# Four layers in one kernel: attention image by image, stacks copied inside SBUF, and a layer on 32x32 tiles

## What is computed

```python
x = x + _L0_conv_ref(_gn(x), W1, W2, bias_w)     # a Volterra convolution, 9 linear and 45 product features
x = x + _L1_conv_ref(_gn(x), weight, bias)       # a convolution by FFT, of the kernel summed over its outputs
x = x + _L2_conv_ref(_gn(x), ...)                # attention in a recurrent cell, below
x = x + _L3_conv_ref(_gn(x), weights1)           # Hartley transform, mix of modes, transform back
```

```python
xin = jnp.einsum('nchw,oc->nohw', x, W_in) + b_in[None, :, None, None]
...
    q = _conv(query, Wq[idx], 'SAME').reshape(n, HEADS, HC, -1)
    k = _conv(token, Wk[idx], 'VALID').reshape(n, HEADS, HC, -1)
    v = _conv(token, Wv[idx], 'VALID').reshape(n, HEADS, HC, -1)
    w = jax.nn.softmax(jnp.einsum('nhcq,nhcd->nhqd', q, k), axis=-1)
    a = jnp.einsum('nhcd,nhqd->nhcq', v, w).reshape(n, CA, hh, ww)
```

## Time and profile before

| engine | busy in us of the span of 337.9 | instructions |
|---|---|---|
| PE, matmul | 311.3 (92%) | 2827 |
| PE, weight load | 120.5 (36%) | 2827 |
| DVE | 208.7 (62%) | 472 |
| ACT | 178.0 (53%) | 337 |
| POOL | 33.4 (10%) | 35 |

### The profile page before, as it was taken

One profiled execution on the slowest core, in us unless ns is written; L12 is line 12 of the kernel. 1 busy time (PEld: TensorE's weight loads), 2 busy tenths in 40 slices (PEclk: granted clock), 3 DMA queues, 4 the chain that ended last, 5 costly groups with the idle time before them and its releaser, 6 DMA issues.

```text
span 337.9 us, 7025 instructions
## 1 busy us (share of the span) xinstructions
PE 311.3 (92%) x2827; PEld 120.5 (36%) x2827; DVE 208.7 (62%) x472; ACT 178.0 (53%) x337; POOL 33.4 (10%) x35
## 2 busy tenths in 40 slices
PE   5999989999988999999999999999999899977793
PEld 1689523234322223323323223322232222423751
DVE  4970362577288337686868878867787221477364
ACT  1100101135185768787887969888788788300400
POOL 6910400000000000100101001010010100000000
PEclk9999978999896569999999999999999999997798
DMA  7000000005650854750000000000000000000001
GB/s 257 31 4 4 2 0 0 3 0 151 161 121 18 157 132 113 278 250 3 2 3 0 3 2 2 0 2 4 2 0 2 2 3 0 0 2 1 4 2 62
DMA packets 3756, 15.05 MB, mean 45 GB/s; under 512 B 804, under 2 KB 1572, under 8 KB 3308
## 3 DMA queue, kind: packets, MB, share of 16 engines
q1 hardware_dynamic: 3468, 14.50, 14.7%
q0 software_dynamic: 256, 0.11, 0.2%
HBM read 12.13 MB, written 2.37 MB: 43 GB/s over the span
## 4 chain that ended last, share of the span: by engine, by line
PE 79%; DVE 12%; issue 4%; ACT 3%; DMA 1%; ACTq 0%; DVEq 0%
PE ps L1151 16%; PE ps L1133 16%; PE ps L1110 15%; PE ps L998 9%; PE ps L1060 3%; PE ps L1254 3%; PE ps L960 2%; PE ps L1048 2%; ACT arena_b L638 2%; PE ps L1156 2%; PE ps L1209 2%; PE ps L1034 2%; PE ps L1026 1%; PE ps L969 1%; DVE arena_a L921 1%
## 5 line engine op out<-in xcount | busy, mean ns | idle before, releaser
L638 ACT ACTIVATE arena_b<-ps 128x512 f32<-128x512 f32 x232 | 125.4, 605 | 32.3 <-PE ps L1133 31.3
L1110 PE MATMUL ps<-arena_a 72*128 72x450 bf16 x256 | 89.3, 378 | 1.4 <-DVE vrest L811 0.8
L1133 PE MATMUL ps<-arena_a 75*128 75x512 bf16 x224 | 86.7, 397 | 0.7 <-ACT arena_b L638 0.3
L846 DVE TENSOR_REDUCE mx<-ps 128x1 f32<-128x450 f32 x120 | 69.3, 618 | 6.8 <-PE ps L1110 5.8
L841 DVE CUSTOM_DVE_ANT_0 sums<-ps,relus 128x450 bf16<-128x450 f32 x68 | 41.3, 626 | 35.7 <-PE ps L1110 29.7
L1151 PE MATMUL ps<-arena_b,vt 128*32 128x512 f32 x448 | 61.4, 621 | 0.7 <-ACT arena_b L638 0.7
L1133 PEld LDWEIGHTS ps<-arena_a 75*128 75x128 bf16 x224 | 21.9, 99 | 72.5 <-ACT arena_b L638 43.9
L646 ACT ACTIVATE relus<-ps 128x450 f32<-128x450 f32 x68 | 37.3, 552 | 7.0 <-PE ps L1110 7.0
L1110 PEld LDWEIGHTS ps<-arena_a 72*128 72x128 bf16 x256 | 24.2, 101 | 36.9 <-DVE mx L841 9.4
L960 PE MATMUL ps<-zeros 128*128 128x512 bf16 x76 | 21.2, 425 | 4.4 <-DMA xa<-x 3.9
L998 PE MATMUL ps<-arena_b,arena_a 32*32 32x512 f32 x720 | 24.6, 610 | 0.0
(11 more groups left out here) (135 smaller groups left out, 240.8 us busy)
## 6 DMA issues: line engine op xcount, KB each, us to landing
arena_b<-wmodes SPq DMA_DIRECT2D x1, 4096.0 KB, 13.3
arena_a<-k_scratch SPq DMA_DIRECT2D x9, 258.4 KB
arena_a<-q_scratch SPq DMA_DIRECT2D x12, 96.0 KB
arena_a<-q_scratch SPq DMA_DIRECT2D x3, 384.0 KB
k_scratch<-arena_b SPq DMA_DIRECT2D x3, 344.5 KB, 3.3
cst<-consts SPq DMA_DIRECT2D x1, 967.5 KB, 7.8
arena_a<-k_scratch SPq DMA_DIRECT2D x6, 129.2 KB
q_scratch<-arena_b SPq DMA_DIRECT2D x6, 128.0 KB, 4.8
```

The source lines that it names most:

```text
L638: nc.scalar.activation(probs[:, n % PRING, :], ps[:, SCORE_RING[n % len(SCORE_RING)], :], ACT.Exp).then_inc(expd, 1)
L846: nc.vector.tensor_reduce(mx[:, a, e:e + 1], bank, AX.X, ALU.max).then_inc(max_read, 1)
L1110: mm(ps[:, block_bank(i), 0:KHALF], qst[0:PAIR_ROWS, e, g, qt * P:(qt + 1) * P], kst[0:PAIR_ROWS, g, at:at + KHALF], start=True, stop=True ...
L1133: last = mm(ps[:, bank, :], kst[0:S_ROWS, g, t * P:(t + 1) * P], qst[0:S_ROWS, e, g, :], start=True, stop=True)
```

## The change

1. **Fillers.** `keep_clock_rows` and `keep_clock_columns` are gone; plain `keep_clock` stands in their places (11 and 8 matmuls). In half 0 each pair of blocks gets one plain filler ahead of it.
2. **Input on 32x32 tiles.** The 24 matmuls of the projection read only the 32 rows of their image. The loop order is now half, row shift, image, so the results of four images end together.
3. **Convolutions.** Keys wait only for the half that they read. Of the values only the first half is convolved ahead of attention; the second half's three pieces stand between the blocks of half 0. Turning the values, their copy (`vs`), the box sums and the gate biases have become items of the plan, behind the blocks of half 0.
4. **Splits.** Keys are split in three ranges instead of two; `xb` is computed behind the queries' split, the identity and the cleared maxima in the second layer.
5. **Stacks from SBUF to SBUF**, one head and one part at a time, without scratch: 12 transfers of keys (24 x 1378 in bf16) and 24 of queries (24 x 512) for an image. The first head's queries are issued by ScalarE. Images 1 to 3 wait for the turns of halves 0 to 2 (`m_in`).
6. **Image by image.** `b, e = divmod(s, 2)`; the first piece of gates waits for seven of eight outputs, not four.
7. **Plan.** 43 items come before the first tile of scores, and 4.35 items of the stream stand in a step; the turn of half 0 is not moved.

```diff
-FIRST_AHEAD = 18
-WIDE_AHEAD = 12
-BLOCKS_PER_STEP = 4.15
+FIRST_AHEAD = 10
+WIDE_AHEAD = 6
+BLOCKS_PER_STEP = 4.35
...
+def image_half(s):
+
+    return divmod(s, 2)
...
-    take(2 * ROWS_OF_MAX + 1 + FIRST_AHEAD)
+    for px in range(3):
+        take(2 * HALF_TILES)
+        plan.append(("v", 1, px))
+    take(2 * HALF_TILES)
+    plan.append(("vs",))
+    take(1)
+    plan.append(("vt",))
+    take(FIRST_AHEAD)
+    plan += [("a2",), ("gb",)]
...
+        def stack_keys(queue, t, b, h):
+
+            r0 = 32 * b + HC * h
+            return queue.dma_start(kst[t * PARTS * HC:(t + 1) * PARTS * HC, b * HEADS + h, :],
+                                   k_parts[r0:r0 + HC, t, :].unsqueeze(1).to_broadcast([HC, PARTS, KW]))
+
+        def stack_queries(queue, t, b, e, h):
+
+            r0 = 32 * b + HC * h
+            return queue.dma_start(qst[t * PARTS * HC:(t + 1) * PARTS * HC, e, b * HEADS + h, :],
+                                   q_parts[r0:r0 + HC, :, e * HALF:(e + 1) * HALF])
...
+            for t, ready in enumerate((k_high, k_mid, k_low)):
+                sp.wait_ge(ready, len(K_RANGES))
+                for h in range(HEADS):
+                    stack_keys(sp, t, 0, h).then_inc(k_first_in[h], 16)
+            sp.wait_ge(q_low, 1)
+            for h in range(1, HEADS):
+                for t in range(PARTS):
+                    stack_queries(sp, t, 0, 0, h).then_inc(q_first_in[h], 16)
...
+            for b in range(1, B):
+                sp.wait_ge(m_in, b * 16)
+                for h in range(HEADS):
+                    for t in range(PARTS):
+                        stack_keys(sp, t, b, h).then_inc(k_in[b - 1], 16)
...
+                if e == 0:
+                    act.wait_ge(q_low, 1)
+                    for t in range(PARTS):
+                        stack_queries(act, t, 0, 0, 0).then_inc(q_first_in[0], 16)
...
             pe.wait_ge(l0_read, 4)
-            keep_clock_rows(3)
+            keep_clock(6, 11)
             pe.wait_ge(padded, 2)
...
             pe.wait_ge(l1_read, 2)
-            keep_clock_columns(6, 1)
-            keep_clock_rows(1)
-            keep_clock_columns(6, 1)
+            keep_clock(6, 8)
             pe.wait_ge(padded, 3)
-            for n in range(2 * B):
-                e, b = divmod(n, B)
+            win = c_("win")
+            for e in range(2):
                 for r in range(3):
-                    last = mm(ps[32 * r:32 * r + 32, (2 + n) % 8, :].rearrange("p (y x) -> p y x", x=W),
-                              c_("win")[:, 32 * b:32 * b + 32],
-                              window(xp, r, 1, 16 * e, 16, W), start=True, stop=True)
-                last.then_inc(xin_done, 1)
...
+                    for b in range(B):
+                        row = slice(32 * b, 32 * b + 32)
+                        n = e * B + b
+                        last = mm(ps[32 * r:32 * r + 32, (2 + n) % 8, :].rearrange("p (y x) -> p y x", x=W),
+                                  win[row, 32 * b:32 * b + 32], window(xp[row], r, 1, 16 * e, 16, W),
+                                  start=True, stop=True)
+                        if r == 2:
+                            last.then_inc(xin_done, 1)
...
+                if s == 0 and i % 2 == 0:
+                    keep_clock(block_bank(i), 1)
+                b, e = image_half(s)
...
+                    if kind == "diff" and s == 0 and a % HALF_TILES == 0:
+                        pe.wait_ge(k_first_in[a // HALF_TILES], PARTS * 16)
+                        pe.wait_ge(q_first_in[a // HALF_TILES], PARTS * 16)
+                    elif kind == "diff" and s > 0 and a == 0:
+                        pe.wait_ge(q_in[s - 1], HEADS * PARTS * 16)
+                        if s % 2 == 0:
+                            pe.wait_ge(k_in[s // 2 - 1], HEADS * PARTS * 16)
...
-                    pe.wait_ge(attn_ready, B if p == 0 else 2 * B)
+                    pe.wait_ge(attn_ready, 2 * B - 1 if p == 0 else 2 * B)
```

393 lines of the change are left out of this document (192 added, 201 removed).

## The result

| | before | after |
|---|---|---|
| median, us | 339.3 (338.15 to 342.02) | 353.56 (351.45 to 355.57) |
| ratio to before | 1 | 1.0408 (95% interval 1.0315 to 1.0501) |
| profiled execution, us | 339.74 | 353.10 |
| its span, us | 337.9 | 351.3 |
| mean granted clock in it | 0.942 | 0.924 |

The changed kernel is **slower by 4.1%**. The forecast was 334.0, its widest range ended at 341, with 0.60 on no change and 0.08 on slower: wrong. A fourth execution of the kernel before, 340.29, has moved its median from 338.3 to 339.3.

The account below looks back on a forecast made before the run. TensorE's work, partly at half clock, was taken to bound the kernel. Terms -2.5 - 5.5 + 1.7 + 1.5 + 0.4 = -4.4 took 339.74 to 335.3 us, 334.0 as median; own range 331 to 337, over all cases 327 to 341.

Parts of the forecast that it names:

- Fillers: Second layer's planes: plain fillers keep full clock, next matmul that counts at 50.55 instead of 53.04 us, -2.5 us.
- input on 32x32 tiles: Third layer's input: 24 matmuls take 1.6 us instead of 6.66; VectorE's evictions end at 67.5 instead of 70.77 us.
- way to the first block: Third layer's input to first block of maxima: 83.2 instead of 93.52 us, 80 to 81 with the fillers' 2.5 off.
- The blocks of the first half image: First block to first score: last block 95.3, turning 97.5, scores from 105.1 instead of 110.62 us, -5.5 us.
- TensorE's gap: TensorE idle from 79.8 to 83.2 us ahead of the first block; clock may fall, +1.7 us (0 to +6).
- first score near 104: Sign that the forecast is right: first tile of scores starts near 104 us.
- these 5.5 us: Gain at the first score, 105.1 instead of 110.62 us, counted in full in the kernel's time.
- The loop: Loop over half images: 8 blocks more at 0.19 us of TensorE each, +1.5; no gain at its half-clock opening.
- What I put at nothing: Loop over eight half images: TensorE's own pace, instructions unchanged but for their order.
- SP's rival: SP's stack issues end last, TensorE waits for image 1; gain gone from about 0.95 us an issue, at worst 351; chance 0.10.
- my estimate from the page's fixed cost: If 24 stack transfers each paid 2.0 us one after the other, 48 us, kernel ends at 361; 0.02 of the 0.10.
- Gates: Loop's end: image by image, the first piece of gates needs half image 6, +0.4 us.

Follow-up runs that it names:

- the run with the sums later: The run beside it (338.37 us), with box sums and gate biases moved from ahead of the first score into the loop's first half: 343.11 us.
- the one beside it: Changed kernel with the big load issued later, 22 fillers ahead of the first block and 10 ahead of the first turning: 338.37 us.
- the two runs with everything at once: Changed kernel with late big load, fillers throughout the front and at the last turning, sums spread in the loop; image 1's keys on POOL 341.48 us, on SP 343.36.

## Why the prediction was wrong, step by step

The profiled execution was forecast 4.4 us shorter and is 13.4 longer. At the end of half 0 the forecast had -6.3 (-2.5, -5.5 and +1.7), and -0.3 came. Behind it, it had +1.9, and +13.7 came. Behind the loop both kernels take 50.4 us.

**Fillers, input on 32x32 tiles, way to the first block: right.** Planes at full clock in 2.15 us (forecast 2.04), the next matmul that counts at 50.12 (50.55); the input's matmuls in 2.21 (within 2.5); the first block at 81.53 (80 to 81).

**"The blocks of the first half image": mis-sized.** From the first block to the first turning I put 14.3 us (83.2 to 97.5), it took 18.8. With the gap filled it took 14.9 (81.56 to 96.50): 3.9 of the 4.5 us are the clock, and "TensorE's gap", which I priced at +1.7 with 0 to +6 around it, is this term. From the turning to the first score I put 7.6 us, it took 11.3; I costed the turned values, ten blocks and the sums at the rates of the earlier trace rows, which are those of a full clock, behind a wait of the kind that had cost the clock before. The first score was forecast near 104 and came at 111.59. My check value in the text, "first score near 104", failed.

**That these 5.5 us would reach the end: wrong.** The end of half 0 came 0.3 us sooner with a first score 1 us later, and again 0.3 us sooner where the first score came 5.8 us sooner (the run with the sums later, against the one beside it). The kernel before spent its time ahead of the first score on 18 blocks, the changed one on ten; what isn't done there is work of TensorE in half 0, and the clock is at half in its first microseconds in every trace read here but three: those of the two runs with everything at once, and that of the old kernel with a filler beside each pair.

**"The loop", +1.5: mis-sized.** I priced eight blocks at 0.19 us of TensorE each. The traces have 179 blocks in halves 1 to 7 instead of 173, and these halves take 4.2 us longer. In halves 1 to 5 it is seven blocks more and 3.2 us, 0.46 us each; half 6 has one fewer and takes 1.0 longer, 0.7 of it the longer wait at the last turn (1.99 and 1.30). The kernel before had a better price than mine: its halves 1 to 5 have 31 or 30 blocks, and those with 31 take 0.36 us more on average. Why a block costs this and not 0.19 is open; idle waits are hardly it, since TensorE is busy for 21.89 of the 22.01 us of such a half.

**What I put at nothing: the step that failed worst.** Of the loop I wrote that "the change leaves its instructions as they are but for their order", and I looked at the stacks' issues only for what waits for them. The load that stands behind them on SP is nobody's bottleneck, and I never asked where it lands when SP is done 58 us later: it met the small transfer on which TensorE waits, 6.3 us, and 2.7 more went at the last turn with the clock, for a reason that stays open.

**SP's rival: right mechanism, wrong victim.** In a row, issues came every 0.72 to 0.97 us, where I put 0.655. That was the length of one issue; in the kernel before, too, three in a row came every 0.70. The price from which I said the gain is gone (0.95) was reached for image 1's keys, not for its 24 issues together (0.90), and image 1 was in time, because the first score was late as well. Its real cost was the lateness of the big load. When the front was made early, the wait for image 1 came (3.48 us). The Trainium skill, "DMA: Bandwidth & Descriptors", section "Rules for kernel authors", speaks for few large transfers; my estimate from the page's fixed cost, 361, did not come, since 36 issues followed one another at 0.81 us (images 2 and 3), and yet the price of making many of them is what moved the big load.

**Gates, +0.4: right.** 0.5, from half 7, with a wait of 0.45 us ahead of them.
